# Output product of the two expert stages, computed feature-major and turned back by two transposes

## What is computed

```python
h1 = jnp.einsum('nd,edf->enf', xf, W1)
h3 = jnp.einsum('nd,edf->enf', xf, W3)
y = jnp.einsum('enf,efd->end', jax.nn.silu(h1) * h3, W2)
...
out = jnp.sum(sel * top_w[:, :, None], axis=1)
```

## Time and profile before

| what | value |
|---|---|
| median of three runs | 1414.75 us |
| the profiled execution, its own time | 1418.55 us |
| its span, first to last instruction | 1416.4 us |
| outside the span | 2.15 us |
| TensorE matmul busy | 1151.2 us (81%) |
| VectorE / ScalarE / GpSimd busy | 911.9 / 718.5 / 746.8 us |
| mean granted TensorE clock | 0.91 of full |

### The profile page before, as it was taken

One profiled execution on the slowest core, in us unless ns is written; L12 is line 12 of the kernel. 1 busy time (PEld: TensorE's weight loads), 2 busy tenths in 40 slices (PEclk: granted clock), 3 DMA queues, 4 the chain that ended last, 5 costly groups with the idle time before them and its releaser, 6 DMA issues. The chain is left out here.

```text
span 1416.4 us, 33456 instructions
## 1 busy us (share of the span) xinstructions
PE 1151.2 (81%) x10358; PEld 1023.1 (72%) x10359; DVE 911.9 (64%) x2572; ACT 718.5 (51%) x1875; POOL 746.8 (53%) x903
## 2 busy tenths in 40 slices
PE   7999999984188888846899999983499999999930
PEld 5887888864188788844676776662499999999930
DVE  4788788864465555514788888755566666666626
ACT  2344344432265555625566666642366666666627
POOL 0266667656446666651146666667244444444446
PEclk9999999986599998977999999985699999999975
DMA  7211112000232222214222112011221111111138
GB/s 230 58 60 45 43 45 71 26 24 31 84 90 88 80 83 82 84 40 141 76 91 84 58 58 75 28 35 58 57 57 53 54 54 56 52 54 54 42 112 266
DMA packets 75408, 102.00 MB, mean 72 GB/s; under 512 B 15154, under 2 KB 51506, under 8 KB 74866
## 3 DMA queue, kind: packets, MB, share of 16 engines
q1 hardware_dynamic: 49586, 60.96, 14.7%
q0 software_dynamic: 17280, 35.69, 7.7%
q10 hardware_dynamic: 8448, 4.20, 1.0%
HBM read 60.93 MB, written 44.11 MB: 74 GB/s over the span
## 5 line engine op out<-in xcount | busy, mean ns | idle before, releaser
L1091 POOL DMA_INDIRECT expert_out<-e_ysb,e_idx x284 | 309.2, 1089 | 309.1 <-ACT e_ysb L1130 180.5
L1239 PE MATMUL banks<-e_x_hi,e_w_hi 128*128 128x256 f32 x852 | 255.9, 300 | 4.6 <-issue 2.4
L1239 PE MATMUL banks<-e_x_hi,e_w_lo 128*128 128x256 f32 x852 | 244.0, 286 | 2.2 <-issue 2.0
L1239 PE MATMUL banks<-e_x_lo,e_w_hi 128*128 128x256 f32 x852 | 243.7, 286 | 2.5 <-issue 2.5
L1249 PE MATMUL banks<-w_dn,e_h 128*128 x1704 | 220.5, 280 | 19.2 <-issue 9.9
L1210 DVE TENSOR_TENSOR e_h<-banks,e_sgl 128x512 f32<-128x512 f32 x213 | 146.8, 690 | 137.0 <-PE banks L1239 75.7
L1249 PEld LDWEIGHTS banks<-w_dn,e_h 128*128 128x128 f32 x1704 | 207.4, 195 | 22.3 <-issue 22.1
L1117 ACT ACTIVATE e_sgl<-banks 128x512 f32<-128x512 f32 x213 | 128.1, 602 | 122.9 <-PE banks L1239 80.0
L1239 PEld LDWEIGHTS banks<-e_x_hi,e_w_hi 128*128 128x128 f32 x852 | 165.9, 195 | 5.8 <-issue 5.7
L1239 PEld LDWEIGHTS banks<-e_x_hi,e_w_lo 128*128 128x128 f32 x852 | 165.5, 194 | 4.7 <-issue 4.7
L1239 PEld LDWEIGHTS banks<-e_x_lo,e_w_hi 128*128 128x128 f32 x852 | 166.0, 195 | 2.8 <-issue 2.6
(11 more groups left out here) (280 smaller groups left out, 2468.7 us busy)
## 6 DMA issues: line engine op xcount, KB each, us to landing
e_xg<-scattered SPq DMA_DIRECT2D x142, 130.0 KB, 1.9
b_cy<-expert_out SPq DMA_DIRECT2D x32, 256.0 KB
f_y<-expert_out SPq DMA_DIRECT2D x32, 256.0 KB, 3.9
expert_out<-e_ysb,e_idx POOLq DMA_INDIRECT x284
a_xT<-in_x_T SPq DMA_DIRECT2D x16, 256.0 KB
out<-f_x ACTq DMA_DIRECT2D x16, 256.0 KB, 4.1
scattered<-in_spare SPq DMA_DIRECT2D x2, 1040.0 KB
scattered<-in_spare SPq DMA_DIRECT2D x16, 130.0 KB
```

What stands on the lines that cost most here:

```text
L1091: nc.gpsimd.indirect_dma_start(out=expert_out, out_offset=bass.IndirectOffsetOnAxis(ap=idx[d.slot][:, i:i + 1], axis=0), in_=ysb[d.slot][: ...
L1239: mm = nc.tensor.matmul(banks[bank_of(j, c)][:, i * ROWS:(i + 1) * ROWS], w_[c.slot][:, g, f:f + P], x_[c.slot][:], start=(k == 0), stop=( ...
```

## The change

The output product is computed feature-major: for each block f of `h` the expert's weights, first copied by ScalarE from `w_dn` into a buffer `w_out` of four, are the stationary operand, and all 256 rows of the tile move. The result (128 features × 256 rows) goes into the second half of the tile's bank YB. VectorE copies it to `yT`, one of two buffers. One step later (lag 7, called e7) TensorE turns it by two transposes into the first half of the same bank, where it stands as before, and signals `y_mm`, on which `idx` and `ysb` wait in the same step. The product itself now signals `yT_mm`. On TensorE the order of a step is b, c, e7, d.

```diff
+                yT = [sb(f"yT{i}", [P, ROWS]) for i in range(2)]
+                w_out = [sb(f"w_out{i}", [P, FC, D]) for i in range(4)]
+                yT_mm, yT_there, w_out_there = sem("yT_mm"), sem("yT_there"), sem("w_out_there")
...
                             if layer == 0 and not (isinstance(d.n, int) and d.n + 1 >= STEPS):
-                                pool.wait_ge(y_mm, d.n + 2)
+                                pool.wait_ge(yT_mm, d.n + 2)
...
                         if c:
+                            e = act.value_load(t_ex[0:1, bass.ds(c.n, 1)], min_val=0, max_val=E - 1)
+                            wait_count(act, yT_mm, c.n - 3)
+                            nc.scalar.copy(w_out[c.slot][:], w_dn[:, bass.ds(e, 1), 0:FC, :].rearrange("p o f d -> p (o f) d")
+                                           ).then_inc(w_out_there, 1)
...
+                        if d:
+                            dve.wait_ge(yT_mm, d.n + 1)
+                            wait_count(dve, y_mm, d.n - 1)
+                            nc.vector.tensor_copy(yT[d.odd][:], YB[d.odd][:, ROWS:]).then_inc(yT_there, 1)
...
-                        if d:
-                            e = pe.value_load(t_ex[0:1, bass.ds(d.n, 1)], min_val=0, max_val=E - 1)
+                        if e7:
+                            pe.wait_ge(yT_there, e7.n + 1)
+                            wait_count(pe, y_there, e7.n - 1)
+                            for i in range(ROWS // P):
+                                mm = nc.tensor.transpose(YB[e7.odd][:, i * D:(i + 1) * D], yT[e7.odd][:, i * P:(i + 1) * P],
+                                                         c_ident[:])
+                            mm.then_inc(y_mm, 1)
+                        if d:
+                            pe.wait_ge(w_out_there, d.n + 1)
                             pe.wait_ge(h_there, PAIRS * d.n + PAIRS)
+                            wait_count(pe, yT_there, d.n - 1)
                             wait_count(pe, y_there, d.n - 1)
-                            for i in range(ROWS // P):
-                                for f in range(FC):
-                                    mm = nc.tensor.matmul(YB[d.odd][:, i * D:(i + 1) * D],
-                                                          h[d.slot][:, f, i * P:(i + 1) * P],
-                                                          w_dn[:, bass.ds(e, 1), f, :].rearrange("p o d -> p (o d)"),
-                                                          start=(f == 0), stop=(f == FC - 1))
-                            mm.then_inc(y_mm, 1)
+                            for f in range(FC):
+                                mm = nc.tensor.matmul(YB[d.odd][:, ROWS:],
+                                                      w_out[d.slot][:, f, :],
+                                                      h[d.slot][:, f, :], start=(f == 0), stop=(f == FC - 1))
+                            mm.then_inc(yT_mm, 1)
-                    run_steps(pe, first if layer else last, last, STEPS, lags, body, unroll=4)
+                    run_steps(pe, first if layer else last, last, STEPS, lags + [7], body, unroll=4)
```

More of the change, by code:

```diff
@@ L1102, in body @@
                     def body(ts):
-                        _, b, c = ts[:3]
+                        _, b, c, _, e7 = ts
                         if b:
@@ L1119, in body @@
                                                      ACT.Silu).then_inc(sg_there, 1)
-                        d = ts[4]
-                        if d:
[L1122 to L1126, removed]
+                        if e7:
+                            act.wait_ge(y_mm, e7.n + 1)
+                            wait_count(act, st[e7.slot], SENT * e7.quarter)
+                            act.wait_ge(at_there, e7.n + 1)
+                            nc.scalar.copy(idx[e7.slot][:], at[:, bass.ds(e7.n, 1), :].rearrange("p o r -> p (o r)")).then_inc(idx_there, 1)
                             if layer:
-                                act.wait_ge(wt_there, d.n + 1)
+                                act.wait_ge(wt_there, e7.n + 1)
                                 for i in range(ROWS // P):
                                     last_i = nc.scalar.activation(
-                                        ysb[d.slot][:, i, :], YB[d.odd][:, i * D:(i + 1) * D], ACT.Copy,
-                                        scale=wt[:, bass.ds(d.n, 1), i:i + 1].rearrange("p o i -> p (o i)"))
+                                        ysb[e7.slot][:, i, :], YB[e7.odd][:, i * D:(i + 1) * D], ACT.Copy,
+                                        scale=wt[:, bass.ds(e7.n, 1), i:i + 1].rearrange("p o i -> p (o i)"))
                                 last_i.then_inc(y_there, 1)
                             else:
-                                nc.scalar.copy(ysb[d.slot][:], YB[d.odd][:, 0:ROWS].rearrange("p (r d) -> p r d", d=D)
+                                nc.scalar.copy(ysb[e7.slot][:], YB[e7.odd][:, 0:ROWS].rearrange("p (r d) -> p r d", d=D)
                                                ).then_inc(y_there, 1)
@@ L1187, in body @@
                     def body(ts):
-                        _, b, c, _ = ts
+                        _, b, c, d = ts
                         if b:
@@ L1220, in body @@
                     def body(ts):
-                        _, b, c, d = ts
+                        _, b, c, d, e7 = ts
                         if b:
```

## The result

The changed kernel takes 1447.86 us, the median of four runs from 1446.21 to 1451.36 us, against 1415.71 us for the kernel before, whose three runs have been joined by a fourth of 1420.02 us. The medians differ by 32 us, or 2.3%. The ratio on record is 1.0191, with a 95% interval from 1.0157 to 1.0224, which would be 27 us; how it weighs the runs isn't told, and 2.3% lies just outside its interval. Each of the four runs is slower than each of the four before, so the kernel is slower for certain; whether by 2% is open. Forecast were 21 us. The time lies inside the range from 1423 to 1458 us, 12 us above the number given, and 2 us above 1446 us, where the forecast's own range ended and the longer ring began. The profiled execution took 1451.36 us, with a span of 1449.5 us, 33.1 us more than before.

A forecast was written before the change was run, and what follows sets the result against it. TensorE was taken to bound experts(1), and a closed loop that stalls now and then experts(0). The terms 11.8 + 8 + 1.3 = +21 us gave 1436 us for the median, with 1423 to 1458 us for 8 in 10.

The forecast's parts named there:

- the forecast's own range: Whole kernel: the main forecast's time, 1428 to 1446 us, given a chance of 0.48.
- the longer ring: Experts(0): late signals pass twice, some 16 stalls cost one us more each atop 13.6 us; 1457 us, chance 0.18.
- Experts(1): TensorE bounds this stage, so its added work counts in full: +0.17 us a tile, +11.8 us over 71 tiles.
- The product's saving: Experts(1): eight wide matmuls take 1.73 us in place of 1.78 for sixteen, saving 0.05 us a tile.
- the transposes: Both expert stages: two more for each tile, priced by their spacing of 0.110 us, add 0.22 us.
- A wide matmul costs as a narrow one: Both expert stages: eight wide matmuls take 0.89 us in experts(1), about 1359 us in all; chance 0.02.
- The copies cost nothing: Both expert stages: ScalarE's weight copy and VectorE's copy to yT fit in free time, in experts(0) if signals come promptly.
- Experts(0): TensorE gets 0.19 us more work a tile, 13.6 us if it sets the pace; somewhat over half shows, +8 us.
- GpSimd hides experts(0): Experts(0): the scatters' 196 us leave the stage as long as it is; 1428 us in all, chance 0.24.
- The stalls go: Experts(0): TensorE's shorter program runs at its free pace of 2.73 us a tile, −27 us; 1401 us, chance 0.06.
- The ends: Copy, two transposes and signals after the last product: +1 us in experts(1), 0.3 in experts(0).

The follow-up runs named there:

- e1_layer1_only: The change made in experts(1) alone, experts(0) as in the kernel before: 1360.98 us, ratio 1.0114 to the kernel before.
- e8_no_turn: The kernel before with the wide product and copied weights in both expert stages, without the copy to yT and turning transposes: 1349.14 us, ratio 1.0008.
- a2_after_again: The changed kernel run again, unedited, on another chip: 1368.23 us beside 1345.91 us for the kernel before, ratio 1.0187.
- e3_work_alone: The kernel before with two extra transposes a tile in experts(0) only, for which nobody waits separately: 1359.57 us, ratio 1.0088.
- e4_all_work: The kernel before with, in experts(0), two extra transposes, ScalarE's weight copy and a VectorE operation a tile, none waited for: 1358.63 us, ratio 1.0099.
- e10: The changed kernel with 2.4 us of VectorE work added ahead of the copy to yT, every fourth step of experts(0): 1393.4 us, ratio 1.0358.
- e9: The kernel before with 2.4 us of VectorE work added at the end of every fourth step of experts(0): 1352.53 us, ratio 1.0048.
- b2_before_again: The kernel before run again, unedited, on another chip: 1344.56 us, ratio 0.9989.

## Why the prediction was right, and where it was not

**Experts(1): right in every term.** Forecast were a period of 5.03 to 5.05 us and +11.8 us; measured are 5.03 and +11.4 (on the second of the experiments' chips again 11.4, and 10.8 in e1_layer1_only). The product's saving was put at 0.05 us and is 0.06; the transposes at 0.22 and are 0.22 (e8_no_turn beside a2_after_again). The duration of 0.27 us that the profile shows for a transpose isn't what it costs. The Trainium skill ("TensorE: Matmul & The Clock Gate", Part 4: PE-mode transpose) gives about 275 ns for a 128×128 transpose in a kernel. As a duration the trace agrees with it, as a cost it doesn't: two of them in e3_work_alone took 0.22 us, not 0.55.

**A wide matmul costs as a narrow one: false.** Eight take 1.73 us, 0.216 each.

**The copies cost nothing: right**, by e4_all_work beside e3_work_alone (216.5 and 216.7 us), where no late signals were.

**Experts(0): the step that failed.** The prediction took +8 us, "somewhat over half" of 13.6, because TensorE ran at 2.54 of 3.16 us a tile and GpSimd finished 24 us after it; part of the added work was to disappear in idle time. The stage took +17.6 us on the first chip and +14.1 on the other, and from first to last transpose it was 243.8 us, outside the 222 to 236 forecast. The idle time covered nothing. On the chips with prompt signals there is none to speak of, and all of the work shows (14.0 us in e3_work_alone). On the first chip the idle time comes from TensorE waiting for others after a late signal, and such a stop starts from the last thing that TensorE has done: work put on TensorE between two stops delays the next one as well. That last reading is argued from the trace; work alone was not run on the first chip. The total fell into the range because the range reached into the ring's case, not because this term was right.

**GpSimd hides experts(0): false.** On the first chip the stage grew by more than the added work; on the other the transposes of rows take 195.8 us with no scatters at all beside 196.5.

**The longer ring: right in its mechanism, and mostly offset in the total.** The stall at 476.37 is as it was described, and there were 33 such waits of 40.7 us, where some 16 were counted. Many are not new: the kernel before lost 39.5 us to the state of the first chip from first to last transpose (221.4 − 181.9), the changed one 47.3 us (243.8 − 196.5), 7.8 more. But that difference is made of two. TensorE's idle time there grew by 38.1 us in place of 23.6, which is 14.5 us more and near the 16 of the rival. Its busy time grew by 9.2 in place of 15.9, 6.7 us less, of which the higher granted clock (0.99 for 0.96) is worth 6 us by the estimate above. The prediction had no term for the clock of experts(0), though its rows have 0.92. Whether the clock was higher by the change or by chance isn't shown. The end of the stage got shorter besides, so of the 7.8 us 17.6 − 14.1 = 3.5 are left by the end of the last scatter. Subtracting across chips rests on one profiled execution of each. That the changed kernel bears a late VectorE worse is shown apart from it, by e10 beside e9.

**The stalls go: false**; TensorE's free pace became 2.73 us as worked out, but the stalls stayed where the signals were late.

**The ends** were put at +1.3 us. From the last transpose to the last scatter, experts(0)'s end got shorter on the first chip, from 25.3 to 20.5 us, which is inside the +17.6; experts(1)'s moved by 0.2 us there (23.7 to 23.9) and by 1.3 on the other chip (22.6 to 23.9).

In sum: 11.4 where 11.8 was forecast, 17.6 for 8 and some tenths, and 3.8 us of the profiled difference in retention1, which the change does not touch and which wanders by more than that in the other runs.

## What to carry to other kernels

An idle share of the engine that does the work is by itself no cover for more of its work: here TensorE was idle for 17% of experts(0), and 13.6 us of added work cost 17.6. Ask first what the idle time waits for. If it is the engine's own signals returning late, as the trace suggests here, added work may be paid in full, and a step that makes one more round trip before the next use of the engine is paid on top; the second was shown with a delay made by hand, the first was not tested where the signals are late. Swapping which operand is stationary in this product left the columns that pass the same and saved 0.02 to 0.06 us a tile; ask first what has to be turned back, and price that by the spacing of such instructions, not by their duration.

## What the runs showed that was not expected

The same program takes 1415.7 us in the first runs and 1344.6 to 1346.8 us on three chips later, 5% less, at a mean granted clock of 0.91 in both profiled executions; in experts(0) alone it is 0.92 and 0.95. Of the 72 us of span, 44.0 lie in experts(0) (246.7 for 202.7). Another 29 are before it, where the first transposes of experts(0) start at 384.9 and at 356.1 us. Experts(1) differs by under 2 us. In experts(0) most of the difference goes with signals of TensorE that arrive late, as where ScalarE waits 4.5 us for one, and with the lower clock; in the runs without such waits, the difference is gone. It is likely so ahead of experts(0) too: there ScalarE waits 39.2 us, 11 times, for releasers that the profile doesn't tell on the first chip, and not once in b2_before_again. What makes the signals late stays open: no experiment met the state of the first runs, and the delayed kernels only imitate one thing that follows from them. Nor is it shown whether the lateness is tied to the chip or to the hour.
